# Gated attention product and BitNet feed-forward on one core: FP8 rounding constants made in one step from absolute values, scales moved into PE's diagonals, all four batches of ctx rounded in PSUM

## The chip, the cores and the metric

One Trainium2 chip, one core. The metric is the device time of one execution in microseconds (us). The kernel before has three timed runs, whose median is 73.7 us (73.02 to 74.86), and one profiled execution. The engines are named as in the profile: PE (TensorE), DVE (VectorE), ACT (ScalarE), POOL (GpSimd) and SP (SyncE, which issues all DMAs here).

## The reference, cut to what matters

Input `x` and `ctx` are 4 batches of 256 rows by 256 columns (f32). What is computed:

```
def fp8(t):                      # amax over the whole tensor
    scale = 448 / max(max|t|, 1e-12)
    return float8_e4m3fn(clip(t * scale, -448, 448)) / scale
xn = (x - mean) / sqrt(var + 1e-5)                     # by row
x  = x + tanh(g_xattn) * (fp8(xn) @ fp8(ctx) + mask)    # 256x256 by 256x256, per batch

def bitlinear(x, w, b):
    xn = (x - mean) * rsqrt(var + 1e-5)
    s  = 127 / max(max|xn| by row, 1e-5)
    xq = clip(round(xn * s), -128, 127) / s
    sw = max(mean|w|, 1e-8)
    return xq @ (clip(round(w / sw), -1, 1) * sw).T + b
h = gelu(bitlinear(layernorm(x), w1, b1))              # 256 -> 1024
x = x + tanh(g_ffn) * bitlinear(h, w2, b2)              # 1024 -> 256
```

## The kernel before, in words

Each batch `b` (0 to 3) is 256 rows, two to a partition (`j` = 0, 1); the hidden stage works on eight tiles `t = 2b + j` of 128 rows by 1024. Five queues are written out by hand, in the order in which each engine takes its calls; a call waits on semaphores, and whatever stands behind it on the same engine waits with it. Two-letter tables (`X_BY`, `CQ_BY`, `MX_BY`, ...) say which engine does a step for which batch: A is ACT, D is DVE, P is POOL.

FP8 rounding is done by adding and taking away a constant of the right size for each element (a "magnet"). Before, the value `v` is scaled first (`x_scaled_a`, L570; `ctx_scaled_a`, L576; `ctx_scaled_d`, L796), then DVE takes its exponent bits (`exponent`, L812), then DVE or POOL lifts them to at least LEAST and multiplies by UP, 2^20 (`magnet_d` L817, `magnet_p` L386). PE adds `v`, the magnet and its negative in PSUM with identity matrices. For x (`x_round`, L1060 to L1062) this also transposes: four blocks of three matmuls, one of them f32. For ctx (`ctx_round`, L1069 to L1071) it is three matmuls of 512 columns, for batches 1 and 2; batches 0 and 3 are rounded by DVE (`ctx_rounded`, L822, L824). ACT copies the results out (`xT_out`, `ctx_out`). `first_product` then multiplies, on top of the mask's rows (`mask_in_rows`), and DVE adds the residual and forms the row sum (`first_residual`, L853).

The scales need the largest value of a whole tensor. DVE reduces (`x_part`, `ctx_part`), PE spreads the parts over all partitions (`spread_x`, `spread_c`, with warm-up matmuls `warm` ahead of each), DVE reduces again, and POOL takes the power -1/2 for x (`x_rows_scale`), DVE the reciprocal for ctx.

Then for each batch: ACT squares, DVE largest (`norm_largest`), POOL `norm_mean` and `norm_floor`, DVE `norm_guard`, POOL the powers (`norm_rows`, L420), the rounding to integers (`norm_round_p` L427 or `norm_round_d` L838), DVE `norm_factor` and POOL `scale_parts` (the bias's factor in three bf16 parts), PE's transposes, and `hidden_product`. For each hidden tile: `gelu` and `squares` on ACT, `hidden_largest` on DVE, `hidden_mean` and `hidden_floor` on POOL, `hidden_guard` on DVE, `hidden_rows` (powers, L465) on POOL by the groups of GROUPS, `hidden_round_p` (L474) on POOL, PE's transposes, copies `hT_out` (DVE or ACT), `out_product`, and `second_residual` on DVE, after which SP stores the tile. The last tile's rounding is split between POOL and DVE. POOL also rounds the weights (`weight_round_p`, L400) and adds the output bias (`residual_out_p`, L448).

Of the kernel before, what the change touches and what calls it, by code (L numbers as in the profile page):

```python
# [27 lines left out]


def gated_fp8_bitnet(nc, x, ctx, mask, g_x, g_f, w1, b1, w2, b2, out):  # L30
# [46 lines left out]
    with ExitStack() as es:  # L77
# [247 lines left out]
        def _(pool):  # L325
# [27 lines left out]
            def x_rows_std():  # L353
                pool.wait_ge(x_ve_done, 1)
                pool.tensor_tensor(x_rstd[:, :, :].rearrange("p b j -> p (b j)"),
                                   x_ve[:, :, :].rearrange("p b j -> p (b j)"), minus_half[:, :], ALU.pow)\
                    .then_inc(x_rstd_done, 1)

            def x_rows_scale():
                pool.wait_ge(amax_x_done, 1)  # L360
                pool.tensor_tensor(scale_x[:, :], amax_x[:, :], minus_half[:, 0:1], ALU.pow).then_inc(scale_x_done, 1)
                pool.wait_ge(scale_x_done, 1)
                pool.wait_ge(x_rstd_done, 1)
                pool.tensor_scalar(x_rs[:, :, :].rearrange("p b j -> p (b j)"),
                                   x_rstd[:, :, :].rearrange("p b j -> p (b j)"), scale_x[:, 0:1], 1.0,
                                   ALU.mult, ALU.mult).then_inc(x_rs_done, 1)
                pool.wait_ge(x_rs_done, 1)
# [918 lines left out]
```

## Time and profile before

| | |
|---|---|
| median of 3 runs | 73.7 us (73.02 to 74.86) |
| profiled execution, its own time | 72.76 us |
| its span, first to last instruction | 71.0 us |
| PE, DVE, ACT, POOL busy | 58.5, 57.1, 50.8, 48.4 us |
| DMA | 5.49 MB, nearly all reads in the first 16 us |

Busy time is counted per engine over the span; register, branch and semaphore instructions aren't in it. Where an engine is blocked inside an instruction, the profile counts that as busy, so a duration that is longer than the same operation's elsewhere is worth a look at what another engine did meanwhile.

### The profile page before, as it was taken

To read this page: it belongs to the slowest core of one execution; us is meant where nothing else is said; L and a number is where in the kernel's file an instruction comes from. 1 tells how busy PE (TensorE), PEld (TensorE's weight loads), DVE (VectorE), ACT (ScalarE), POOL (GpSimd) and SP (SyncE) were. 2 spreads that over 40 slices of the span, in tenths; PEclk is the share of its full clock that TensorE was granted. 3 is DMA by queue.
4 is the path that set the end of the run, shared out by engine and by line. 5 is a ranking of instruction groups with operands and counts; after the bars stand their busy time and mean duration, and the time that the engine had idled before them with its cause. 6 is when DMAs were issued, how large, how long until landed. Compare 5 with 4: busy or idle time off the path is not lost. (4 is left out here: it accounts for less than half of the span.)

```text
span 71.0 us, 1599 instructions
## 1 busy us (share of the span) xinstructions
PE 58.5 (83%) x523; PEld 39.5 (56%) x528; DVE 57.1 (80%) x133; ACT 50.8 (72%) x108; POOL 48.4 (68%) x90
## 2 busy tenths in 40 slices
PE   0069999988932899999998998999979999978850
PEld 0069999755931495936383342522756548856730
DVE  1339999778999855989949899469999999999850
ACT  5169922899993475195999797999859997975400
POOL 4012167679999986689996869799507898988100
DMA  0999999951000000000000000000002002102232
GB/s 2 259 247 368 321 327 370 404 158 6 3 1 0 0 0 18 0 0 0 0 5 0 0 0 0 0 0 9 0 0 74 0 0 83 60 14 74 79 133 84
DMA packets 6191, 5.49 MB, mean 77 GB/s; under 512 B 2084, under 2 KB 5544, under 8 KB 6184
## 3 DMA queue, kind: packets, MB, share of 16 engines
q1 hardware_dynamic: 6184, 5.40, 24.6%
q8 instruction: 4, 0.07, 0.4%
q14 instruction: 3, 0.02, 0.1%
HBM read 4.33 MB, written 1.05 MB: 76 GB/s over the span
## 5 line engine op out<-in xcount | busy, mean ns | idle before, releaser
L1020 PE MATMUL p_h<-ident_b 128*128 128x128 bf16 x143 | 10.7, 243 | 4.2 <-DVE x_sum L709 4.2
L1020 PEld LDWEIGHTS p_h<-ident_b 128*128 128x128 bf16 x143 | 10.2, 111 | 4.9 <-issue 4.9
L878 DVE TENSOR_REDUCE h_mx<-h_sqv 128x1 f32<-128x1024 f32 x8 | 9.7, 1206 | 0.0
L621 ACT ACTIVATE h<-p_h,s_f 128x1024 f32<-128x1024 f32 x8 | 8.8, 1103 | 1.0 <-PE p_h L1129 0.9
L474 POOL TENSOR_SCALAR hq<-h,h_nm,h_ar 128x1024 int16<-128x1024 f32 (+1 forms) x8 | 9.1, 1139 | 0.4
L629 ACT ACTIVATE h_sqv<-h,h_sum 128x1024 f32<-128x1024 f32 x8 | 9.1, 1141 | 0.1
L1128 PE MATMUL p_h<-w1T,x1qT 128*128 128x512 bf16 x29 | 9.0, 382 | 0.1
L1060 PE MATMUL p_X<-ident_f,v 128*128 128x128 f32 x32 | 6.4, 301 | 0.2 <-DVE magnet L817 0.2
L465 POOL TENSOR_TENSOR h_ar<-h_ge,minus_half 128x4 f32<-128x4 f32 (+1 forms) x5 | 4.5, 896 | 2.9 <-DVE h_ge L884 2.8
L448 POOL TENSOR_TENSOR y<-x,b_gate 128x256 f32<-128x256 f32 x8 | 6.2, 791 | 0.2
L1129 PE MATMUL p_h<-b_rows,uT 9*128 9x512 bf16 x16 | 6.2, 384 | 0.1
L812 DVE TENSOR_SCALAR magnet<-v 128x512 int16<-128x512 int16 x8 | 4.7, 596 | 1.8 <-ACT v L576 1.3
L400 POOL TENSOR_SCALAR wq<-w_sb,w_inv 128x1024 int16<-128x1024 f32 x4 | 5.6, 1412 | 0.7 <-DVE w_inv L769 0.6
L554 ACT ACTIVATE x_sqv<-x_sb,x_sum 128x256 f32<-128x256 f32 x8 | 4.0, 497 | 2.2 <-DVE x_sum L709 2.1
L560 ACT ACTIVATE w_junk<-w_sb 128x1024 bf16<-128x1024 f32 x4 | 4.2, 1050 | 1.7 <-DMA w_sb<-in_L_ffn_w_dram 1.7
L1060 PEld LDWEIGHTS p_X<-ident_f,v 128*128 128x128 f32 x32 | 4.9, 190 | 0.8 <-DVE magnet L817 0.4
L1129 PEld LDWEIGHTS p_h<-b_rows,uT 9*128 9x128 bf16 x16 | 1.4, 90 | 6.8 <-issue 6.8
L606 ACT ACTIVATE s_sqv<-x,s_sum 128x256 f32<-128x256 f32 x8 | 4.0, 501 | 1.1 <-DVE x L853 1.1
L838 DVE TENSOR_SCALAR x1q<-x,s_nm,s_ar 128x256 int16<-128x256 f32 x6 | 3.9, 685 | 1.0 <-POOL s_ar L420 1.0
L1191 PE MATMUL p_A<-w2T,hqT 128*128 128x256 bf16 x32 | 4.2, 273 | 0.5 <-DVE hqT L909 0.5
L339 POOL TENSOR_SCALAR x_nm<-x_sum 128x2 f32<-128x2 f32 x4 | 0.8, 192 | 5.4 <-DVE x_sum L709 3.7
L1079 PE MATMUL p_A<-mask_s,rows_sel 4*128 4x512 f32 x8 | 4.4, 626 | 0.0
(125 smaller groups left out, 153.5 us busy)
## 6 DMA issues: line engine op xcount, KB each, us to landing
w_sb<-in_L_ffn_w_dram SPq DMA_DIRECT2D x4, 512.0 KB, 6.1
ctx_sb<-in_ctx_dram SPq DMA_DIRECT2D x4, 256.0 KB, 4.8
out_dram<-y SPq DMA_DIRECT2D x8, 128.0 KB, 1.7
x_sb<-in_x_dram SPq DMA_DIRECT2D x3, 256.0 KB, 3.7
x_sb<-in_x_dram SPq DMA_DIRECT2D x2, 128.0 KB, 2.2
b_rows<-b_parts SPq DMA_DIRECT2D x9, 2.0 KB, 2.2
b_sb<-in_L_ffn_b_dram SPq DMA_DIRECT2D x1, 128.0 KB, 7.6
b_sb<-in_L_ffn_b_dram SPq DMA_DIRECT2D x1, 4.0 KB, 4.9
```

Source lines behind the costliest of these rows:

```text
L400: pool.tensor_scalar(wq[:, m, n * F:(n + 1) * F], flat, w_inv[:, m:m + 1], 1.0, ALU.mult, ALU.mult)\
L448: pool.tensor_tensor(y[:, b, j], x1[:, b, j], b2_gate[:, :], ALU.add).then_inc(x1b_done["P"], 1)
L465: pool.tensor_tensor(h_ar[:, lo:hi].rearrange("p t e -> p (t e)"), h_ge[:, lo:hi].rearrange("p t e -> p (t e)"), minus_half[:, 0:2 * (hi - ...
L474: pool.tensor_scalar(hq[:, t % HB, 0:cols], h[:, t, 0:cols], h_nm[:, t:t + 1], h_ar[:, t, 0:1], ALU.add, ALU.mult).then_inc(hq_done["P"], 1)
L621: nc.scalar.activation(h[:, t], p_h[t % 2][:, :, :].rearrange("p a n -> p (a n)"), ACT.Gelu, scale=s_f[:, t // J, t % J:t % J + 1], accum_ ...
L629: nc.scalar.activation(h_sqv[:, t % SQ], h[:, t], ACT.Square, bias=h_sum[:, t:t + 1], scale=-float(F), accum_out=h_sq[:, t:t + 1]).then_in ...
L812: V.tensor_scalar(magnet[:, b % 2, m].bitcast(I16), high, EXP_BITS, MANT_HALF, ALU.bitwise_and, ALU.bitwise_or).then_inc((exp_x_done, exp_ ...
L878: V.tensor_reduce(h_mx[:, t:t + 1], h_sqv[:, t % SQ], AX.X, ALU.max).then_inc(h_mx_done, 1)
L1020: M.matmul(bank[:, 0:P], ident_b[:, :], ident_b[:, :], start=True, stop=True)
L1060: M.matmul(p_X[:, part], v[:, b, 0, part], ident_f[:, :], start=True, stop=False)
L1128: M.matmul(p_h[t % 2][:, n], x1qT[:, b, j, k], w1T[:, k, cols], start=(k == 0), stop=False)
L1129: mm = M.matmul(p_h[t % 2][:, n], uT[:, b, j], b1_rows[:, cols], start=False, stop=True)
```

## The change

- The magnet is made in one operation: absolute value (by ACT, or by DVE as a bit mask) of x normed or of ctx as loaded, in bf16 (`size`), times the scale, at least LEAST. The factor UP moves into PE's constants (`up_b`, `nup_b`), the scale into diagonal matrices (`diag_x`, `diag_c`) that take the place of the f32 identity. `xn` is x normed but not scaled, by POOL for batches 0 and 3, ACT for 1, DVE for 2.
- All batches of ctx go through `ctx_round` and `ctx_out`; `ctx_rounded` isn't called.
- x's variances and their powers come in two halves; the floor of amax is an added element of `x_ratio`.
- `norm_guard`, `norm_factor`, `hidden_guard` and `hidden_factor` use `tensor_scalar` by column where they used two tensor operands.
- Weight roundings: three of four go to DVE. `norm_round` of batches 1 and 2 goes to POOL. `hT_out(3)` goes to ACT. The first hidden group is split into two.
- The orders of the four compute queues are written anew.

The core of the diff, with the helpers of each engine:

```
-EXP_BITS = 0x7F80
-MANT_HALF = 0x0040
+NO_SIGN = 0x7FFF
 UP = float(2**20)
+LEAST_AMAX = (FP8_EPS / FP8_MAX) ** 2
...
-    GROUPS = ((0, 2), (2, 4), (4, 6), (6, 7), (7, 8))
-    HEAD_WARM = 95
-    X_BY = "AAAA"
-    C_BY = "DAAA"
-    CQ_BY = "DAAD"
-    W_BY = "PPPP"
-    NR_BY = "PDDD"
-    MX_BY = "DDDD"
-    MC_BY = "PPDD"
+    GROUPS = ((0, 1), (1, 2), (2, 4), (4, 6), (6, 7), (7, 8))
+    HEAD_WARM = 68
+    X_BY = "PADP"
+    SX_BY = "AADA"
+    SC_BY = "AAAA"
+    CQ_BY = "AAAA"
+    W_BY = "PDDD"
+    NR_BY = "PPPD"
+    MX_BY = "DDPP"
+    MC_BY = "PPPD"
-    WO_BY = "DDAD"
+    WO_BY = "ADAD"
...
 (POOL)
-            def magnet_p(b, m):
-                pool.wait_ge((exp_x_done, exp_c_done)[m], b + 1)
-                pool.tensor_scalar(magnet[:, b % 2, m], magnet[:, b % 2, m], LEAST, UP, ALU.max, ALU.mult)
+            def x_normed_p(b):
+                pool.wait_ge(x_rstd_done, b // XH + 1)
+                pool.wait_ge(x_nm_done, b + 1)
+                for j in range(J):
+                    pool.tensor_scalar(xn[:, b, j * D:(j + 1) * D], x_sb[:, b, j], x_nm[:, b, j:j + 1], x_rstd[:, b, j:j + 1],
+                                       ALU.add, ALU.mult).then_inc(xn_done["P"], 1)
+            def x_scale():
+                pool.wait_ge(raw_x_done, 1)
+                pool.tensor_tensor(scale_x[:, :], amax_raw[:, 0:1], minus_half[:, 0:1], ALU.pow).then_inc(scale_x_done, 1)
+            def magnet_x_p(b):
+                pool.wait_ge(scale_x_done, 1)
+                pool.wait_ge(size_x_done[SX_BY[b]], nth(SX_BY, b))
+                if b >= 2:
+                    pool.wait_ge(xT_psum, b - 1)
+                pool.tensor_scalar(magnet[:, b % 2, 0], size[:, b, 0], scale_x[:, 0:1], LEAST, ALU.mult, ALU.max)\
+                    .then_inc(magnet_done[0]["P"], 1)
...
 (ACT)
+            def size_x_a(b):
+                act.wait_ge(xn_done[X_BY[b]], J * nth(X_BY, b))
+                nc.scalar.activation(size[:, b, 0], xn[:, b], ACT.Abs).then_inc(size_x_done["A"], 1)
+            def size_c_a(b):
+                act.wait_ge(ctx_in[b], 16)
+                nc.scalar.activation(size[:, b, 1], ctx_sb[:, b].rearrange("p k d -> p (k d)"), ACT.Abs)\
+                    .then_inc(size_c_done["A"], 1)
...
 (DVE)
-            V.tensor_scalar(nident_b[:, :], ident_f[:, :], -1.0, None, ALU.mult)
+            V.tensor_scalar(up_b[:, :], ident_f[:, :], UP, None, ALU.mult)
+            V.tensor_scalar(nup_b[:, :], ident_f[:, :], -UP, None, ALU.mult)
...
+            def diagonal_x():
+                dve.wait_ge(scale_x_done, 1)
+                V.tensor_scalar(diag_x[:, :], ident_f[:, :], scale_x[:, 0:1], None, ALU.mult).then_inc(diag_x_done, 1)
...
+            def size_x_d(b):
+                dve.wait_ge(xn_done[X_BY[b]], J * nth(X_BY, b))
+                V.tensor_scalar(size[:, b, 0].bitcast(I16), high_half(xn[:, b]), NO_SIGN, None, ALU.bitwise_and)
...
-                high = v[:, b, m].bitcast(I16).rearrange("p (n e) -> p n e", e=2)[:, :, 1]
-                V.tensor_scalar(magnet[:, b % 2, m].bitcast(I16), high, EXP_BITS, MANT_HALF,
-                                ALU.bitwise_and, ALU.bitwise_or).then_inc((exp_x_done, exp_c_done)[m], 1)
...
             def norm_guard(b):
-                V.scalar_tensor_tensor(out=s_ge[:, b, 0], in0=s_mx[:, b], scalar=1.0 / (float(D) * Q_MAX) ** 2,
-                                       in1=s_ge[:, b, 1], op0=ALU.mult, op1=ALU.max).then_inc(s_g_done, 1)
+                for j in range(J):
+                    V.tensor_scalar(s_ge[:, b, 0, j:j + 1], s_mx[:, b, j:j + 1], 1.0 / (float(D) * Q_MAX) ** 2,
+                                    s_ge[:, b, 1, j:j + 1], ALU.mult, ALU.max).then_inc(s_g_done, 1)
...
 (PE)
-                    M.matmul(p_X[:, part], v[:, b, 0, part], ident_f[:, :], start=True, stop=False)
-                    M.matmul(p_X[:, part], magnet[:, b % 2, 0, part], ident_b[:, :], start=False, stop=False)
-                    mm = M.matmul(p_X[:, part], magnet[:, b % 2, 0, part], nident_b[:, :], start=False, stop=True)
+                    M.matmul(p_X[:, part], xn[:, b, part], diag_x[:, :], start=True, stop=False)
+                    M.matmul(p_X[:, part], magnet[:, b % 2, 0, part], up_b[:, :], start=False, stop=False)
+                    mm = M.matmul(p_X[:, part], magnet[:, b % 2, 0, part], nup_b[:, :], start=False, stop=True)
...
-                M.matmul(p_C, ident_f[:, :], v[:, b, 1], start=True, stop=False)
+                M.matmul(p_C, diag_c[:, :], ctx_sb[:, b].rearrange("p k d -> p (k d)"), start=True, stop=False)
+                M.matmul(p_C, up_b[:, :], magnet[:, b % 2, 1], start=False, stop=False)
+                M.matmul(p_C, nup_b[:, :], magnet[:, b % 2, 1], start=False, stop=True).then_inc(c_psum, 1)
...
-            warm(16, p_h[1][:, 1])
+            warm(38, p_h[1][:, 1])
             spread_c()
-            warm(18, p_h[1][:, 1])
+            x_round(0)
```

The new orders, as far as the prediction speaks of them:

```
POOL: x_mean(0..3), x_rows_std(0), x_normed_p(0), bias_parts, x_scale, x_rows_std(1), x_normed_p(3), magnet_c_p(0),
  mask_scaled, x_rows_shift, magnet_c_p(1), magnet_x_p(2), gated_bias, weight_round_p(0,0), magnet_c_p(2), norm_mean(0),
  residual_out_p(0), norm_floor(0), magnet_x_p(3), norm_rows(0), norm_round_p(0), scale_parts(0), residual_out_p(1),
  norm_floor(1), norm_mean(1), norm_rows(1), residual_out_p(2), norm_round_p(1), scale_parts(1), norm_mean(2),
  norm_floor(2), hidden_mean(0), hidden_mean(1), hidden_floor(0), norm_rows(2), norm_round_p(2), scale_parts(2),
  hidden_rows(0), hidden_round_p(0), ..., hidden_round_p(6), hidden_rows(5), hidden_round_p(7)
ACT: ..., x_squares(3), size_c_a(0), size_c_a(1), gates_tanh, size_c_a(2), size_x_a(0), weight_abs(0,0), size_c_a(3),
  weight_abs(0,1), weight_abs(1,0), xT_out(0), weight_abs(1,1), ctx_out(0), x_normed_a(1), size_x_a(1), size_x_a(3),
  norm_squares(0), weight_out_a(0,0), ctx_out(1), ..., gelu(7), hT_out(3), squares(7), hT_out(4), ...
DVE: ..., x_part, ctx_largest(1), largest_x, ctx_largest(2), ctx_largest(3), diagonal_x, ctx_part, magnet_x_d(0),
  largest_c, diagonal_c, unscaling, x_normed_d(2), size_x_d(2), weight_scale(0), weight_round_d(0,1), weight_scale(1),
  first_residual(0), magnet_x_d(1), weight_round_d(1,0), weight_round_d(1,1), norm_largest(0), norm_guard(0),
  magnet_c_d(3), norm_factor(0), first_residual(1), ...
PE: warm(68), spread_x, warm(38), spread_c, x_round(0), weight_sums(0), ctx_round(0), mask_in_rows(0),
  weight_sums(1), first_product(0), ctx_round(1), weight_T(0,0), x_round(1), mask_in_rows(1), x_round(2),
  first_product(1), ctx_round(2), mask_in_rows(2), norm_T(0), weight_T(0,1), first_product(2), scale_T(0),
  weight_T(1,0), weight_T(1,1), hidden_product(0), hidden_product(1), ctx_round(3), norm_T(1), x_round(3),
  scale_T(1), mask_in_rows(3), first_product(3), norm_T(2), hidden_product(2), ...
```

Warm matmuls in the hidden stage are 14, 19, 6 and 4 where they were 5, 12, 15, 10 and 3.

## Rows read from the trace of the kernel before

**Rows 1.** The page: busy time by engine, and the weight roundings on POOL.
```profile
PE 58.5 (83%) x523; PEld 39.5 (56%) x528; DVE 57.1 (80%) x133; ACT 50.8 (72%) x108; POOL 48.4 (68%) x90
...
L400 POOL TENSOR_SCALAR wq<-w_sb,w_inv 128x1024 int16<-128x1024 f32 x4 | 5.6, 1412 | 0.7 <-DVE w_inv L769 0.6
```

**Rows 2.** The chain that ended last: start us, us, what.
```profile
64.30 0.67 POOL h_ar L465
```

**Rows 3.** List of waits: waiting group, releaser, us in total, times, longest.
```profile
POOL h_ar L465 <- DVE h_ge L884: 2.8, 2, 2.6
...
POOL u_parts L435 <- DVE s_u L874: 1.3, 3, 0.5
...
POOL wq L400 <- DVE w_inv L769: 0.6, 1, 0.6
...
POOL magnet L386 <- DVE magnet L812: 0.4, 1, 0.4
```

**Rows 4.** Timeline of POOL: start us, us, line, operation, and idle before it.
```profile
12.87 0.55 POOL L361 TENSOR_TENSOR scale_x<-amax_x,minus_half 128x1 f32<-128x1 f32 x1 [0.53 <-DVE amax_x L743]
...
13.53 0.28 POOL L364 TENSOR_SCALAR x_rs<-x_rstd,scale_x 128x8 f32<-128x8 f32 x1
...
25.66 1.04 POOL L420 TENSOR_TENSOR s_ar<-s_ge,minus_half 128x4 f32<-128x4 f32 x1
...
26.82 1.09 POOL L427 TENSOR_SCALAR x1q<-x,s_nm,s_ar 128x256 int16<-128x256 f32 x2
...
31.10 0.66 POOL L439 CAST u_parts<-s_rest 128x6 bf16<-128x6 f32 x1
...
47.28 2.37 POOL L474 TENSOR_SCALAR hq<-h,h_nm,h_ar 128x1024 int16<-128x1024 f32 x2
...
61.76 0.70 POOL L465 TENSOR_TENSOR h_ar<-h_ge,minus_half 128x2 f32<-128x2 f32 x1
...
62.83 1.19 POOL L474 TENSOR_SCALAR hq<-h,h_nm,h_ar 128x1024 int16<-128x1024 f32 x1
...
65.07 0.77 POOL L474 TENSOR_SCALAR hq<-h,h_nm,h_ar 128x512 int16<-128x512 f32 x1
```

**Rows 5.** The tile magnet: duration ns min/median/max, first and last start us.
```profile
L386 POOL TENSOR_SCALAR magnet<-magnet x2: 1918/1922/1927, 15.2 to 21.4; 128x512 bf16<-128x512 bf16 x2
...
L812 DVE TENSOR_SCALAR magnet<-v x8: 410/478/1259, 14.6 to 32.7; 128x512 int16<-128x512 int16 x8
...
L817 DVE TENSOR_SCALAR magnet<-magnet x6: 275/372/714, 16.6 to 34.5; 128x512 bf16<-128x512 bf16 x6
...
L822 DVE TENSOR_TENSOR v<-v,magnet x2: 672/682/692, 17.2 to 30.3; 128x512 f32<-128x512 f32 x2
...
L824 DVE TENSOR_TENSOR cq<-v,magnet x2: 691/1090/1490, 17.9 to 31.0; 128x512 bf16<-128x512 f32 x2
```

**Rows 6.** Two source lines of DVE, s_f and x1q: columns as in rows 5.
```profile
L872 DVE TENSOR_TENSOR s_f<-s_t,s_ar x4: 160/161/1061, 29.7 to 47.4; 128x2 f32<-128x2 f32 x4
...
L838 DVE TENSOR_SCALAR x1q<-x,s_nm,s_ar x6: 395/616/1201, 36.4 to 49.7; 128x256 int16<-128x256 f32 x6
```

**Rows 7.** Timeline of DVE: columns as in rows 4.
```profile
21.93 0.47 DVE L853 SCALAR_TENSOR_TENSOR x<-p_A,coef,x_sb 128x256 f32<-128x256 f32 x1
...
28.48 0.47 DVE L853 SCALAR_TENSOR_TENSOR x<-p_A,coef,x_sb 128x256 f32<-128x256 f32 x1
...
63.12 0.91 DVE L884 SCALAR_TENSOR_TENSOR h_ge<-h_mx,h_ge 128x1 f32<-128x1 f32 x1
```

**Rows 8.** Timeline of PE: columns as in rows 4.
```profile
4.18 7.39 PE L1020 MATMUL p_h<-ident_b 128*128 128x128 bf16 x95 [4.18 <-DVE x_sum L709]
...
17.35 0.49 PE L1060 MATMUL p_X<-ident_f,v 128*128 128x128 f32 x2 [0.24 <-DVE magnet L817]
...
23.32 1.12 PE L1069 MATMUL p_hT<-v,ident_f 128*128 128x512 f32 x2 [1.56 <-POOL magnet L386]
...
42.74 0.38 PE L1129 MATMUL p_h<-b_rows,uT 9*128 9x512 bf16 x1
```

More of the change, by code:

```diff
@@ L47, in gated_fp8_bitnet @@
     SQ = 3
+    XH = 2
     HT = 4
@@ L351, in bias_parts, with x_rows_std @@
                 pool.tensor_copy(b1_parts[:, 2], b1_rest[:, 1]).then_inc(b1_ready, 1)
[L353 to L367, printed above, removed]
+            def x_rows_std(i):
+                part = slice(i * XH, (i + 1) * XH)
+                pool.wait_ge(x_ve_done, i + 1)
+                pool.tensor_tensor(x_rstd[:, part].rearrange("p b j -> p (b j)"), x_ve[:, part].rearrange("p b j -> p (b j)"),
+                                   minus_half[:, 0:XH * J], ALU.pow).then_inc(x_rstd_done, 1)
@@ L480, in _ @@
             x_mean(3)
-            x_rows_std()
+            x_rows_std(0)
+            x_normed_p(0)
             bias_parts()
-            x_rows_scale()
+            x_scale()
+            x_rows_std(1)
+            x_normed_p(3)
+            magnet_c_p(0)
             mask_scaled()
-            magnet_p(0, 1)
+            x_rows_shift()
+            magnet_c_p(1)
+            magnet_x_p(2)
+            gated_bias()
             weight_round_p(0, 0)
-            weight_round_p(0, 1)
-            gated_bias()
@@ L489, in _ @@
-            magnet_p(1, 1)
+            magnet_c_p(2)
+            norm_mean(0)
             residual_out_p(0)
             norm_floor(0)
-            norm_mean(0)
+            magnet_x_p(3)
             norm_rows(0)
             norm_round_p(0)
-            weight_round_p(1, 0)
             scale_parts(0)
-            weight_round_p(1, 1)
+            residual_out_p(1)
+            norm_floor(1)
             norm_mean(1)
-            norm_floor(1)
-            residual_out_p(1)
             norm_rows(1)
+            residual_out_p(2)
@@ L502, in _ @@
+            norm_round_p(1)
+            scale_parts(1)
+            norm_mean(2)
             norm_floor(2)
[L503 to L504 removed]
+            hidden_mean(0)
+            hidden_mean(1)
+            hidden_floor(0)
             norm_rows(2)
[L506 removed]
+            norm_round_p(2)
             scale_parts(2)
[L508 to L512 removed]
@@ L513, in _ @@
-            hidden_rows(0)
-            norm_rows(3)
-            hidden_mean(1)
-            hidden_round_p(0)
-            hidden_round_p(1)
-            scale_parts(3)
-            hidden_floor(1)
-            hidden_rows(1)
-            hidden_mean(2)
+            hidden_rows(0)
+            hidden_round_p(0)
+            norm_floor(3)
+            hidden_floor(1)
+            norm_mean(3)
+            norm_rows(3)
+            hidden_rows(1)
+            hidden_round_p(1)
+            hidden_mean(2)
@@ L691, in _ @@
             gelu(7)
+            hT_out(3)
             squares(7)
```

376 lines of the change are left out of this document (196 added, 180 removed).

## The prediction

> **What bounds the kernel now.** I read the page first [rows 1]: PE and DVE are busiest at 83% and 80%, ACT 72%, POOL 68%, and no engine is full, so no single one explains 71.0 us. Then the chain of waits. It is short; what it shows is the end [rows 2]: the last row statistics on POOL start at 64.30 and release the last rounding, the last transposes and the last output products. So the end is set by when POOL gets to `hidden_round_p(7)`. The list of waits and POOL's timeline give the reason. POOL is in-order, and from `x_scale` at 12.87 us to the end of the last rounding at 65.84 [rows 4] it has seven waits: 0.4, 0.6, three of 1.3 together and two of 2.8 together [rows 3], 5.2 by the unrounded timeline. Its 53.0 us there are thus 47.8 us of work. The other limiter is DVE, which hands POOL its inputs: the longest wait, 2.6 us, is for `hidden_guard(1)`, behind a DVE queue that runs back to back.
>
> The DVE rows also show a lock between the two. `s_f` (two operands in SBUF, 2 elements) takes 0.16 us alone and 1.06 us when it starts 0.1 us into a POOL rounding; `x1q` is 0.40 alone and up to 1.20 [rows 6, 4]. The last guard takes 0.91 and ends at 64.03, as `hidden_round_p(6)` does [rows 7, 4].
>
> **The change, by part, on each queue.**
>
> DVE loses eight exponents (median 0.48) and six `magnet_d` (median 0.37), of which three shorter ones come back (0.3) [rows 5]: 3.8 + 2.2 - 0.9 us. It loses both `ctx_rounded`, whose second halves are 0.69 and 1.49 [rows 5] and the first about 0.7 each: 3.6. Two of three `norm_round_d` pairs go, 2 x 2 x 0.62 [rows 6]: 2.5, and `hT_out(3)` and one `ctx_scaled_d`, about 1.0. It gains three weight roundings of 1024 elements; the 256-element `x1q` is 0.40 alone, the 1024 by the same 2 elements a cycle about 0.8, so 2.4 (up to 1.9 each if POOL holds the port); `x_normed_d(2)` 0.8, `size_x_d(2)` 0.4, and some six small diagonals and copies, 1.0. Net -7.6 us, most of it before 36 us; on the path it is worth only what DVE was late for. Guards and factors take the form with one SBUF tensor and scalars. I cost them at 0.17 however POOL stands, and if I am wrong they stay at up to 0.9. The last one saves 0.2 only, since POOL was in `hidden_round_p(6)` until 64.02 and started the row statistics at 64.30 [rows 4, 2].
>
> PE: `ctx_round` for batches 0 and 3 is new, 1.4 us each by the spacing of the one at 23.32 [rows 8]; x rounding keeps its twelve matmuls. The first runs where PE waits now, the other between `hidden_product(1)` and `(2)`. Warm-up ahead of `spread_x` falls from 95 matmuls in 7.39 us [rows 8] to 68 in 5.3, ending at 9.4; `spread_x` now waits for `x_part`, which I put at 10.8. The 38 behind it end at 14.1 and hold up `spread_c` (`ctx_part` is there at 13.3), so ctx's scale moves from 13.7 to 15.2. The x side gains: `x_round(0)` needs only `scale_x` and starts near 14.4, not 17.35 [rows 8].
>
> ACT gives three `ctx_scaled_a` and six x rows (4.9) for seven Abs copies (4.4), of which five need no scale and lie in its idle time ahead of the weight sums. It gains `ctx_out(0)`, `ctx_out(3)`, `weight_out_a(0, 0)` (0.5, 0.5, 0.9) and `hT_out(3)`, 1.0 us between `gelu(7)` and `squares(7)`. `hidden_round_p(6)` on POOL hides the last as long as POOL is the later one; with POOL early it is what is late next. SP's order stays; `bias_parts`, which releases its nine row copies, ends near 12.3 in both.
>
> POOL is where I make the sum, start to start:
> - `x_rows_std(0)` from 8.75 (1.0), `x_normed_p(0)` 1.1, `bias_parts` 1.35, so `x_scale` starts at 12.35, not 12.87: -0.5;
> - `x_rows_std(1)` 1.1 and `x_normed_p(3)` 1.1 (durations of `s_ar` and `x1q` [rows 4]), less `x_rs` 0.36: +1.8;
> - five magnets where there were two, 1.92 [rows 5] and 0.08 between starts: +6.0;
> - one weight rounding where there were four in 5.6 us [rows 1]: -4.5;
> - `norm_round_p(1)` and `(2)`: +2 x 1.15 = +2.3 [rows 4];
> - the first hidden group split, two powers of 0.70 [rows 4] for one of 1.03, and one more mean and floor: +1.0.
>
> That is +6.1. Against it stand the 5.2 us of waits, which must all vanish. I followed the queues: POOL reaches `norm_mean(0)` at 26.3, its input is there at 22.0; `norm_rows(0)` at 30.5, guard ready at 28.6; `norm_rows(1)` 36.2; `norm_rows(2)` 42.5; `hidden_round_p(0)` 46.7 (before 47.28 [rows 4]). I found no wait. So +0.9 to +1.0: the last rounding ends near 66.8, and what follows it is as before.
>
> **The disputed price** is a POOL magnet. The nearest row is `magnet_p`: same shape, same types, also a maximum and a product, 1.92 us both times [rows 5]. The other bound comes from POOL's f32 roundings: 0.77 for 512 elements, 0.55 for 256, 1.19 for 1024 [rows 4]. The new form has the product first and a scale from SBUF, as they do. I take 1.92 since shape, types and the maximum are shared; both ends stay in the range.
>
> The rows show 1.92 us for 512 bf16 elements. The Trainium skill ("GPSIMD Engine Reference", section 3.1) gives about 1.8 cycles an element in the best case, 769 ns for 512 elements. By it five magnets would cost 3.8 and not 9.6. This case's magnet row disagrees with it, its f32 row agrees.
>
> **Conversion.** The profiled execution took 72.76 us for its span of 71.0. The median of the three runs is 73.7, 1.3% above. +1.0 gives 73.8, and at the same ratio 74.7.
>
> **Rivals.**
> 1. *POOL magnets are cheap* (0.77, 5 x 1.15 less, so POOL's queue could end 4.8 earlier than now). Then `magnet_c_p(0)` ends at 16.1, `first_product(0)` at 19.5, `first_residual(0)` starts at 19.6 against 21.93 [rows 7]. POOL doesn't bound any more: `squares(7)` behind the moved `hT_out(3)`, and PE's hidden products with 43 warm matmuls, put the last rounding near 62.5, -3.3. The weight roundings collide with POOL on the port, so I take -2.8: 70.0 profiled, 70.9. For it: the f32 rows. Against: the magnet row.
> 2. *Slower: the magnet ahead of `norm_rows(0)`.* `magnet_x_p(3)` stands in POOL's queue between `norm_floor(0)` and `norm_rows(0)`. At 2.0 us each `norm_rows(0)` starts at 30.5 where it was 25.66 [rows 4]. On DVE `norm_factor(0)` waits for it with `first_residual(1)` behind, 32.1 against 28.48 [rows 7]. PE's `mask_in_rows(2)` waits for that; `hidden_product(0)` and `(1)` end at 37.9 and 39.6, then `ctx_round(3)`, `x_round(3)`, mask and product (4.5 us) lie before `hidden_product(2)`, which ends at 46.6 against 43.1 [rows 8]. If the hidden stage then keeps its old pace and absorbs nothing, it is +3.5 less 0.7 from unlocked guards: 75.6, or 76.6. It decides from the point where POOL waits over 0.5 us in total after 48 us. For it: the old stage had the 2.6 us wait. Against: the sum leaves POOL no time to wait in.
> 3. *It does little*: DVE's two-operand work no longer holds POOL up (`u_parts` is 0.66 beside it [rows 4]), about 1.0 us back from POOL's durations, which cancels the sum: 73.7.
>
> That lock is by instruction in the rows: 0.16 becomes 1.06. The Trainium skill ("SBUF — State Buffer", on the shared pair) says whichever of a DVE 2-port operation and a GpSimd one starts first holds it throughout. That speaks against weight roundings on DVE beside POOL's magnets. In the trace DVE's magnets range from 0.28 to 0.71 [rows 5], so a collision costs up to what POOL has left.
>
> **How the numbers follow.** Forecast 74.7: 0.35, its own range 73.4 to 76.0. Rival 1, 70.9: 0.32; I give it that much since one differing operand may put the new form on the cheap side. Rival 2, 76.6: 0.25. Rival 3, 73.7: 0.08. A difference under 2% (72.2 to 75.2) can't be told from none here. Faster: nearly all of rival 1 and a little of the forecast, 0.34. Slower: most of rival 2 and the upper part of the forecast, 0.31. Within: the rest, 0.35. The range reaches to both ends: 70.2 to 76.9.
>
> **What would show it.** POOL's magnet rows: 1.9 or 0.8. `x_scale` at 12.4, `x_round(0)` at 14.4, `norm_rows(0)` at 30.5 (rival 1: about 25), `hidden_product(2)` ending at 46.6 or 40.6. POOL's waits after 13 us: near none in the forecast, over 0.5 in rival 2. The last guard at 0.2. Wrong would be a first `x_round` later than 15.5, or a queue held up by ACT's Abs copies, which I costed at nothing.

## The result, and the profile after

The changed kernel took 78.75 us (median of four runs, 78.06 to 79.24), the kernel before 73.36 (72.94 to 74.86) in the runs beside it: a ratio of 1.0725 [1.064, 1.0811]. It is 7% slower, beyond the range of the prediction. Runs of one kernel differ by some per cent with the granted clock, so each ratio here and below compares only the least disturbed runs of both sides, while medians and ranges are of all runs. The profiled execution took 78.55 us for a span of 76.4. The mean granted clock of TensorE (1.00 is 2.4 GHz throughout) was 0.933 in every run of it; in the profiled run of before it was 1.00.

The page of the changed kernel: span, busy times, the row of the granted clock in 40 slices, and the costliest group that is new.

```profile
span 76.4 us, 1564 instructions
...
PE 64.1 (84%) x492; PEld 40.7 (53%) x497; DVE 49.4 (65%) x140; ACT 52.6 (69%) x110; POOL 54.4 (71%) x101
...
PEclk9999999999555699999569999999999999999999
...
L400 POOL TENSOR_SCALAR magnet<-size,scale_c 128x512 bf16<-128x512 bf16 x3 | 6.6, 2186 | 0.3
```

Against [rows 1]: DVE did lose its work (57.1 to 49.4 us), POOL took on 6.0 us, and PE's busy time rose by 5.6 us, though it has 31 matmuls fewer (492). The clock row has two dents, one in slices 11 to 14 and one in 20 and 21.

POOL's timeline (start, duration, instruction; in brackets the idle time before it and who ended it).

```profile
12.76 0.56 POOL L382 TENSOR_TENSOR scale_x<-amax_raw,minus_half 128x1 f32<-128x1 f32 x1
...
15.60 2.07 POOL L400 TENSOR_SCALAR magnet<-size,scale_c 128x512 bf16<-128x512 bf16 x1
...
18.95 1.99 POOL L400 TENSOR_SCALAR magnet<-size,scale_c 128x512 bf16<-128x512 bf16 x1
21.03 1.99 POOL L389 TENSOR_SCALAR magnet<-size,scale_x 128x512 bf16<-128x512 bf16 x1
...
24.78 2.50 POOL L400 TENSOR_SCALAR magnet<-size,scale_c 128x512 bf16<-128x512 bf16 x1
...
29.30 1.99 POOL L389 TENSOR_SCALAR magnet<-size,scale_x 128x512 bf16<-128x512 bf16 x1
31.38 1.03 POOL L433 TENSOR_TENSOR s_ar<-s_ge,minus_half 128x4 f32<-128x4 f32 x1
...
37.25 1.03 POOL L433 TENSOR_TENSOR s_ar<-s_ge,minus_half 128x4 f32<-128x4 f32 x1 [0.73 <-DVE s_ge L922]
...
44.03 0.19 POOL L466 TENSOR_SCALAR h_nm<-h_sum 128x1 f32<-128x1 f32 x1 [1.52 <-ACT h L646]
45.16 0.19 POOL L471 TENSOR_SCALAR h_ge<-h_sq 128x1 f32<-128x1 f32 x1 [0.94 <-ACT h_sqv L654]
45.44 1.03 POOL L433 TENSOR_TENSOR s_ar<-s_ge,minus_half 128x4 f32<-128x4 f32 x1
...
49.41 1.20 POOL L487 TENSOR_SCALAR hq<-h,h_nm,h_ar 128x1024 int16<-128x1024 f32 x1
...
58.81 1.03 POOL L478 TENSOR_TENSOR h_ar<-h_ge,minus_half 128x4 f32<-128x4 f32 x1 [1.29 <-DVE h_ge L945]
...
70.29 1.03 POOL L487 TENSOR_SCALAR hq<-h,h_nm,h_ar 128x512 int16<-128x512 f32 x1
```

Three things are to be seen. The five magnets take 2.0 to 2.5 us each. From 13.3 to 36.5 us POOL has no wait at all, so whatever stands in its queue ahead of `norm_rows(0)` is paid in full: that starts at 31.38, against 25.66 [rows 4]. And from 36.5 on POOL does wait: 0.73, 1.52, 0.94 and 1.29, together 4.5 us. The last rounding starts 5.2 later than before (70.29 against 65.07 [rows 4]), which is nearly all of the 5.4 us by which the span grew.

How the lateness travels is on the other queues. DVE's timeline:

```profile
15.92 0.82 DVE L838 TENSOR_SCALAR xn<-x_sb,x_nm,x_rstd 128x256 f32<-128x256 f32 x2
...
32.45 0.45 DVE L929 TENSOR_SCALAR s_t<-s_ge,s_ar 128x1 f32<-128x1 f32 x2 [2.31 <-POOL s_ar L433]
...
33.29 0.48 DVE L911 SCALAR_TENSOR_TENSOR x<-p_A,coef,x_sb 128x256 f32<-128x256 f32 x1
```

and PE's:

```profile
14.18 0.40 PE L1115 MATMUL p_X<-diag_x,xn 128*128 128x128 f32 x2
...
17.81 1.10 PE L1125 MATMUL p_hT<-ctx_sb,diag_c 128*128 128x512 f32 x2 [0.83 <-POOL magnet L400]
...
19.31 2.07 PE L1135 MATMUL p_A<-mask_s,rows_sel 4*128 4x512 f32 x2
...
34.33 1.09 PE L1135 MATMUL p_A<-mask_s,rows_sel 4*128 4x512 f32 x2 [1.92 <-DVE x L911]
...
37.12 1.89 PE L1103 MATMUL p_h<-ident_b,wq 128*128 128x128 bf16 x16
...
42.32 0.39 PE L1185 MATMUL p_h<-b_rows,uT 9*128 9x512 bf16 x1
...
49.34 0.39 PE L1185 MATMUL p_h<-b_rows,uT 9*128 9x512 bf16 x1
```

`norm_factor(0)` on DVE waits 2.31 us for POOL's `s_ar`, with `first_residual(1)` behind it: 33.29 against 28.48 [rows 7]. `mask_in_rows(2)` on PE waits 1.92 us for that. `hidden_product(2)` ends at 49.7 against 43.1 [rows 8].

The same two `mask_in_rows` matmuls take 2.07 us at 19.31 and 1.09 at 34.33: the first run at half the clock. Windows of the changed kernel (start:end, us; busy us and instructions of PE, PEld, DVE, ACT and POOL; granted clock; DMA share; GB/s):

```profile
13.00:36.50 23.50, 20.13 (x126) 12.56 (x124) 12.39 (x41) 13.97 (x29) 21.96 (x28) 0.85 0.16 50
...
20.00:22.00 2.00, 2.00 (x6) 0.69 (x5) 0.00 (x0) 1.97 (x5) 1.91 (x2) 0.50 0.03 1
...
34.00:40.00 6.00, 5.67 (x39) 3.35 (x39) 3.56 (x13) 4.34 (x11) 4.95 (x11) 0.72 0.02 4
```

From 13.0 to 36.5 PE did 126 matmuls in 20.1 us busy at a mean clock of 0.85; before had 165 in 19.93 at 1.00. A busy share read without the clock column would make PE look loaded, when it was slow. Ahead of the first fall (2.4 to 1.2 GHz) PE had worked little between 15.9 and 17.8 us, waiting 0.52 us for a weight's absolute values and 0.83 for the first ctx magnet; ahead of the second it had waited 1.92 us.

So two theories stand for what comes after: the POOL magnets lengthen an unbroken queue and the rest follows (theory 1), or the clock makes much of the loss itself (theory 2). A third is that it matters where one magnet stands (rival 2's `magnet_x_p(3)` just ahead of `norm_rows(0)`).

### The profile page after: what moved, and what is told of

The parts are those of the page before. It is cut to its first block, busy times and chain, and to the rows that moved or that the text cites. A ratio compares the mean times of both kernels' runs of the same rounds, so it can differ in the third digit from the quotient of the medians.

```text
span 76.4 us, 1564 instructions
## 1 busy us (share of the span) xinstructions
PE 64.1 (84%) x492; PEld 40.7 (53%) x497; DVE 49.4 (65%) x140; ACT 52.6 (69%) x110; POOL 54.4 (71%) x101
## 4 chain that ended last, share of the span: by engine, by line
PE 42%; POOL 21%; issue 11%; DMA 9%; SPq 7%; DVE 3%; ACT 2%; POOLq 2%
PE p_h L1184 11%; DMA w_sb<-in_L_ffn_w_dram 9%; PE p_h L1185 7%; POOL magnet L400 6%; POOL magnet L389 3%; PE p_h L1103 3%; PE p_A L1135 3%; POOL hq L487 3%; PE p_X L1074 3%; PE p_X L1247 2%; PE p_A L1247 2%; SPq L310 2%; POOL h_ar L478 2%; PE p_hT L1196 2%; SPq L308 2%
## 5 line engine op out<-in xcount | busy, mean ns | idle before, releaser
L1074 PE MATMUL p_h<-ident_b 128*128 128x128 bf16 x106 | 8.5, 257 | 4.3 <-DVE x_sum L742 4.3
L1074 PEld LDWEIGHTS p_h<-ident_b 128*128 128x128 bf16 x106 | 8.2, 118 | 4.2 <-issue 4.2
L1135 PE MATMUL p_A<-mask_s,rows_sel 4*128 4x512 f32 x8 | 5.4, 760 | 1.9 <-DVE x L911 1.9
L400 POOL TENSOR_SCALAR magnet<-size,scale_c 128x512 bf16<-128x512 bf16 x3 | 6.6, 2186 | 0.3
L1115 PE MATMUL p_X<-diag_x,xn 128*128 128x128 f32 x32 | 6.4, 302 | 0.0
L1125 PE MATMUL p_hT<-ctx_sb,diag_c 128*128 128x512 f32 x8 | 5.2, 732 | 0.8 <-POOL magnet L400 0.8
L478 POOL TENSOR_TENSOR h_ar<-h_ge,minus_half 128x2 f32<-128x2 f32 (+1 forms) x6 | 4.9, 811 | 1.3 <-DVE h_ge L945 1.3
L461 POOL TENSOR_TENSOR y<-x,b_gate 128x256 f32<-128x256 f32 x8 | 5.6, 725 | 0.0
L1115 PEld LDWEIGHTS p_X<-diag_x,xn 128*128 128x128 f32 x32 | 4.8, 191 | 0.8 <-issue 0.8
L433 POOL TENSOR_TENSOR s_ar<-s_ge,minus_half 128x4 f32<-128x4 f32 x4 | 4.1, 1028 | 0.9 <-DVE s_ge L922 0.7
```

Source lines behind the costliest of these rows:

```text
L400: pool.tensor_scalar(magnet[:, b % 2, 1], size[:, b, 1], scale_c[:, 0:1], LEAST, ALU.mult, ALU.max).then_inc(magnet_done[1]["P"], 1)
L478: pool.tensor_tensor(h_ar[:, lo:hi].rearrange("p t e -> p (t e)"), h_ge[:, lo:hi].rearrange("p t e -> p (t e)"), minus_half[:, 0:2 * (hi - ...
L1074: M.matmul(bank[:, 0:P], ident_b[:, :], ident_b[:, :], start=True, stop=True)
L1115: M.matmul(p_X[:, part], xn[:, b, part], diag_x[:, :], start=True, stop=False)
L1135: M.matmul(p_A[:, :, :], rows_sel[:, b], mask_s[:, :].rearrange("b (o n) -> b o n", o=1).broadcast_to([B, J, D]), start=True, stop=True)
```

## Experiments

Each ratio is against runs of the kernel before on the same chip.

**1. All magnets on DVE.** Everything else of the change stays.

```diff
-    MX_BY = "DDPP"
-    MC_BY = "PPPD"
+    MX_BY = "DDDD"
+    MC_BY = "DDDD"
-            magnet_c_p(0)        # and the four others in POOL's queue
+            magnet_c_d(0)        # at the same places of DVE's
```

> The changed kernel with its four POOL magnets of batch 0 to 2 of ctx and two of x (five in all) made by DVE; nothing else. POOL theory: five operations of 2.0 us each stand in POOL's in-order queue, four of them ahead of the row statistics of batch 0 and one right before them; without them norm_rows(0) starts near 25 us instead of 31.4, the second half of hidden_product for tile 2 ends near 43 instead of 49.7, and the time falls from 78.6 by 5 to 7 us, to 72 to 74. Clock theory (PE at half clock from 19 to 26 and 36 to 39 us is what costs): PE still waits between x_round(0) and the mask, the clock falls as before, and no more than 3 us come back.

70.38 us (70.13 to 70.99), ratio 0.9656 [0.95, 0.9812]: faster than before, by 1.9 to 5.0%. It is 8.4 us below the change (7.8 by the ratios), more than either theory expected. Its timeline, POOL and DVE:

```profile
24.93 1.05 POOL L433 TENSOR_TENSOR s_ar<-s_ge,minus_half 128x4 f32<-128x4 f32 x1 [2.51 <-DVE s_ge L917]
...
30.82 1.03 POOL L433 TENSOR_TENSOR s_ar<-s_ge,minus_half 128x4 f32<-128x4 f32 x1 [0.75 <-DVE s_ge L917]
...
37.18 0.19 POOL L471 TENSOR_SCALAR h_ge<-h_sq 128x1 f32<-128x1 f32 x1 [0.94 <-ACT h_sqv L649]
...
50.80 1.03 POOL L478 TENSOR_TENSOR h_ar<-h_ge,minus_half 128x4 f32<-128x4 f32 x1 [1.29 <-DVE h_ge L940]
...
62.24 1.03 POOL L487 TENSOR_SCALAR hq<-h,h_nm,h_ar 128x512 int16<-128x512 f32 x1
...
14.84 0.40 DVE L865 TENSOR_SCALAR magnet<-size,scale_c 128x512 bf16<-128x512 bf16 x1
```

What takes POOL 2.0 us takes DVE 0.4. `norm_rows(0)` comes 6.5 us earlier than in the change, and POOL now waits 2.5 us ahead of it; the clock stays at 1.00 and `hidden_product(2)` ends at 41.7. So the loss goes with where these five instructions are done, and the rest of the change is worth 3.4%. As the clock came back too, this run doesn't separate theories 1 and 2. Three of the changed kernel's waits on POOL are there too (0.75, 0.94, 1.29), though POOL is 6.5 us earlier.

**2. What a POOL magnet costs.** The kernel before, with eight forms of 128x512 `tensor_scalar` at the end of POOL's queue, where the output is being finished.

```diff
+  (t_bo, t_b, sc, LEAST, ALU.mult, ALU.max),     # bf16 -> bf16, the change's form
+  (t_bo, t_b, LEAST, UP, ALU.max, ALU.mult),     # the form of before
+  (t_bo, t_b, sc, 1.0, ALU.mult, ALU.mult),      # no maximum
+  (t_bo, t_f, sc, LEAST, ALU.mult, ALU.max),     # f32 -> bf16
+  (t_fo, t_f, sc, LEAST, ALU.mult, ALU.max),     # f32 -> f32
+  (t_fo, t_f, ...mult, mult), (t_bo, t_f, ...mult, mult), (t_fo, t_b, ...mult, mult)
```

> The kernel before, with eight tensor_scalar operations of 128x512 on scratch tiles behind POOL's last rounding, one after the other: (1) bf16 to bf16, scale times then maximum (the new magnet); (2) bf16 to bf16, maximum then times, both immediates (the old one); (3) bf16 to bf16, times and times; (4) f32 to bf16, times then maximum; (5) f32 to f32, times then maximum; (6) f32 to f32, times and times; (7) f32 to bf16, times and times; (8) bf16 to f32, times and times. If the maximum makes it slow: 1, 2, 4, 5 take 1.9 to 2.0 us and 3, 6, 7, 8 take 0.77. If the bf16 input does: 1, 2, 3, 8 are slow. If the bf16 output does: 1, 2, 3, 4, 7 are slow. Its output is the reference's; its time means nothing.

The eight in this order; the fifth and sixth share a row.

```profile
67.37 2.05 POOL L505 TENSOR_SCALAR t_bo<-t_b,t_s 128x512 bf16<-128x512 bf16 x1
69.51 1.93 POOL L505 TENSOR_SCALAR t_bo<-t_b 128x512 bf16<-128x512 bf16 x1
71.54 0.69 POOL L505 TENSOR_SCALAR t_bo<-t_b,t_s 128x512 bf16<-128x512 bf16 x1
72.33 2.00 POOL L505 TENSOR_SCALAR t_bo<-t_f,t_s 128x512 bf16<-128x512 f32 x1
74.42 2.78 POOL L505 TENSOR_SCALAR t_fo<-t_f,t_s 128x512 f32<-128x512 f32 x2
77.29 0.69 POOL L505 TENSOR_SCALAR t_bo<-t_f,t_s 128x512 bf16<-128x512 f32 x1
78.08 0.69 POOL L505 TENSOR_SCALAR t_fo<-t_b,t_s 128x512 f32<-128x512 bf16 x1
```

The first, second, fourth and fifth have a maximum and take 1.93 to 2.05 us (the fifth alone 1.99); the four without take 0.69, whatever the types. The prediction's two bounds (1.92 from a magnet row, 0.77 from an f32 rounding) differ by the operation and not by the type. Only one shape was tried.

**3. The change without the maximum**, magnets still on POOL (the floor `LEAST` is left out, so tiny inputs are rounded otherwise).

```diff
-  pool.tensor_scalar(magnet[...], size[...], scale[:, 0:1], LEAST, ALU.mult, ALU.max)
+  pool.tensor_scalar(magnet[...], size[...], scale[:, 0:1], 1.0, ALU.mult, ALU.mult)
```

> The changed kernel with every queue as it is; the five POOL magnets only multiply (times scale, times 1.0), the maximum with LEAST is left out, so that the smallest elements are rounded too finely. In the row of forms such an operation took 0.69 us where the one with the maximum took 2.05. If the price of the maximum on POOL is the cause: POOL's queue loses 5 x 1.35 = 6.8 us ahead of the second x rounding and the row statistics, PE's gaps close, the granted clock goes back to 1.00, and the time is that of the version with all magnets on DVE or little above it, 70 to 72. If the placement of the operations on POOL (the lock, the order) costs, most of the 5 us stays lost, 75 or more.

71.89 us (70.93 to 72.31), ratio 0.9778 [0.9703, 0.9854], at a clock of 1.00.

```profile
15.72 0.69 POOL L400 TENSOR_SCALAR magnet<-size,scale_c 128x512 bf16<-128x512 bf16 x1
...
25.40 0.69 POOL L389 TENSOR_SCALAR magnet<-size,scale_x 128x512 bf16<-128x512 bf16 x1 [1.91 <-PE p_X L1117]
26.06 1.05 POOL L433 TENSOR_TENSOR s_ar<-s_ge,minus_half 128x4 f32<-128x4 f32 x1
```

Nothing moves and no order changes; only the price does, and the time falls by 6.9 us, more than the loss. The queue is broken again (a wait of 1.91 us), and PE's waits of 0.83 for the magnet and 1.92 for `x` are gone. With experiments 1 and 2 this shows the cause: the price of the maximum on POOL, times five.

**4. One magnet off POOL: the last or the first.**

```diff
-    MX_BY = "DDPP"                 -    MC_BY = "PPPD"
+    MX_BY = "DDPD"                 +    MC_BY = "DPPD"
-            magnet_x_p(3)          -            magnet_c_p(0)
```

> The changed kernel with magnet_x(3) alone on DVE, behind norm_guard(0); the other four stay on POOL. POOL theory: one operation of 2.0 us less in a queue without a wait up to norm_rows(0), which starts 2.0 earlier (29.4); PE's gap ahead of the mask of batch 2 shrinks from 1.9 us to under 1. 76.0 to 76.8, 1.8 to 2.5 us faster. Clock theory: the first stretch at half clock stays as it is and is most of the loss, so under 1.5 us.

> The changed kernel with magnet_c(0) alone on DVE, behind diagonal_c; the other four stay on POOL. POOL theory: again 2.0 us less in the same unbroken queue, the same 76.0 to 76.8 as with the last magnet moved, though it is another place. Clock theory: this one closes the wait of PE for ctx_round(0) in front of the first stretch at half clock, so it gives clearly more than the last magnet: 75 or less.

Without the last: 75.78 us at a clock of 0.974. Its other runs, at 0.955, 0.933 and 0.934, took 77.35 to 79.1, so no ratio is given; the two at the changed kernel's own clock were no faster than it (79.06 and 79.1 against 78.06 to 79.24). Without the first: 76.94 (75.75 to 77.85), ratio 1.0426 [1.0373, 1.0479], at 0.954 to 0.955.

`norm_rows(0)` starts at 29.60 and 29.17, so 1.8 and 2.2 us before 31.38; 0.4 and 0.5 of that is an earlier `x_scale` (12.36 and 12.23, against 12.76). For this start the place just ahead of `norm_rows(0)` is no worse than the first: each magnet counts with about its length, as it must in a queue without a wait. That is theory 1; the third theory falls. The end doesn't follow so simply. The last rounding starts at 67.74 and 69.59, so 2.6 and 0.7 us before 70.29: in the second profiled execution PE ran at half clock from 32 to 39 us, on the matmuls behind `first_residual(1)`, and that took most of the gain back.

**5. The clock held by spare matmuls.** Two tries. Spare matmuls, whose results nothing reads, go behind `x_round(0)` (10) and `weight_sums(0)` (16), where PE waits, and ahead of `mask_in_rows(2)` (26); the second try has 36 there and 38 more ahead of `weight_T(0, 0)`.

```diff
+            warm(10, p_h[1][:, 1])      # behind x_round(0)
+            warm(16, p_h[1][:, 1])      # behind weight_sums(0)
+            warm(38, p_h[1][:, 1])      # ahead of weight_T(0, 0), second try only
+            warm(26, p_h[1][:, 1])      # ahead of mask_in_rows(2); 36 in the second try
```

> The changed kernel with 10 warm-up matmuls behind x_round(0), 16 behind weight_sums(0) and 26 ahead of mask_in_rows(2), in PE's gaps. If they hold the clock at 1.00 throughout: clock theory says 3 to 4.5 us come back (sum of what PE's rows grew by: about 2.8 in the first stretch, 1.6 in the second), 74 to 75.5. POOL theory says that the first stretch is hidden, since POOL has no wait between 13.3 and 36.5 us, and only the second counts: 1.0 to 1.6 us back, about 77.3.

The first missed: 78.33 us (76.54 to 80.99), and the clock still fell in all but one run (the 76.54). In the profiled one it fell behind a wait of 2.83 us for a weight rounding that I had left uncovered:

```profile
24.96 0.62 PE L1103 MATMUL p_h<-ident_b,wq 128*128 128x128 bf16 x8 [2.83 <-POOL wq L413]
27.84 2.07 PE L1135 MATMUL p_A<-mask_s,rows_sel 4*128 4x512 f32 x2
```

> The changed kernel with warm-up matmuls in all four gaps of PE: 10 behind x_round(0), 16 behind weight_sums(0), 38 ahead of weight_T(0, 0), 36 ahead of mask_in_rows(2). The earlier try left the 2.8 us gap ahead of weight_T(0, 0) open and the clock fell behind it. With the clock at 1.00 throughout: POOL theory 1.5 to 2.2 us back (only the stretch behind 36 us lies on the path; one execution of the earlier try that kept 1.00 took 76.5), 76.4 to 77.1. Clock theory: 4 us or more, 74.5 or less.

The second kept 1.00 in every run: 77.13 us (76.97 to 77.43), ratio 1.0592 [1.0555, 1.0629]. Its POOL timeline:

```profile
12.44 0.56 POOL L382 TENSOR_TENSOR scale_x<-amax_raw,minus_half 128x1 f32<-128x1 f32 x1
...
31.32 1.03 POOL L433 TENSOR_TENSOR s_ar<-s_ge,minus_half 128x4 f32<-128x4 f32 x1
...
47.81 1.20 POOL L487 TENSOR_SCALAR hq<-h,h_nm,h_ar 128x1024 int16<-128x1024 f32 x1
...
68.69 1.03 POOL L487 TENSOR_SCALAR hq<-h,h_nm,h_ar 128x512 int16<-128x512 f32 x1
```

`norm_rows(0)` is where it was (31.32 against 31.38), so the first stretch at half clock was hidden behind POOL. The first hidden rounding and the last both start 1.6 us earlier: the second stretch cost about 1.5, and POOL's wait of 1.52 us for gelu is gone with it. By the ratios the clock is worth 1.0 us (1.0725 less 1.0592, times 73.4; by the ends of the two intervals 0.1 to 1.9). Theory 2 holds for a fifth to somewhat over a quarter of the loss of 5.3 us.

**6. The small forms alone.** The kernel before with the change's guards and factors (one SBUF tensor and scalars).

```diff
-  V.scalar_tensor_tensor(out=s_ge[:, b, 0], in0=s_mx[:, b], scalar=..., in1=s_ge[:, b, 1], ...)
+  for j in range(J):
+      V.tensor_scalar(s_ge[:, b, 0, j:j + 1], s_mx[:, b, j:j + 1], ..., s_ge[:, b, 1, j:j + 1], ...)
   # factors, hidden guards and hidden factors likewise
```

> The kernel before, with the row guards and factors of both norms in the form of the change (tensor_scalar, one column at a time, one SBUF tensor) and nothing else. My costing: each is 0.17 us however POOL stands, so the guards that took 0.86 and 0.91 shrink, and 0.2 us or a little more is gained, 73.2 against 73.4. If the new form is held by POOL too, or two instructions for a pair cost what the lock gave, no gain: 73.4 or up to 0.5 more.

74.96 us (73.89 to 77.26), ratio 1.0145 [0.9889, 1.0401]: unclear, with no gain to be seen. The single-column guards were 0.20 to 0.21, but the factor of two columns with one SBUF tensor reached 0.84 (`s_f`) and 0.48 (`h_f`) beside POOL roundings, against 0.23 elsewhere.

**7. A better order.** From experiment 1: DVE's `norm_largest(0)` and `norm_guard(0)` ahead of the second weight's roundings; on PE `first_product(1)` ahead of `x_round(2)` and `norm_T(0)` ahead of `ctx_round(2)` (ACT's copies in the same order); POOL's `norm_rows(2)` and its rounding ahead of the first hidden means, and DVE's `norm_factor(2)` ahead of `hidden_largest(0)`. The diff shows POOL's part.

```diff
             norm_round_p(1) ...                     # POOL
+            norm_rows(2)
+            norm_round_p(2)
             hidden_mean(0), hidden_mean(1), hidden_floor(0)
-            norm_rows(2)
-            norm_round_p(2)
```

> The version with all magnets on DVE, and these orders: norm_largest(0) and norm_guard(0) ahead of the two roundings of w2 on DVE (POOL waited 2.5 us for that guard); first_product(1) ahead of x_round(2) and norm_T(0) ahead of ctx_round(2) on PE, ACT's copies in the same order; norm_rows(2) ahead of the first hidden means and floor on POOL. If POOL's waits for guards set the pace between 22 and 40 us: the second half of hidden_product for tile 2 ends 1 to 2 us earlier than 41.7, 68.5 to 69.5 against 70.4. If PE's own queue sets it (no gap from 21 us on but 1.5 us), nothing is gained, 70.0 to 70.7.

69.37 us (68.85 to 72.01), ratio 0.946 [0.9355, 0.9564]: with experiment 9's the best version of this study, 4.4 to 6.5% under the kernel before. The last rounding starts at 61.39, not 62.24. Against experiment 1 it gains about 1 us (1.4 by the ratios, whose intervals overlap). What each of the orders gave is open.

**8. Batch 3 of ctx back to DVE**, from experiment 1, and with experiment 7's order.

```diff
-    CQ_BY = "AAAA"
+    CQ_BY = "AAAD"
+            ctx_rounded(3)      # DVE
-            ctx_round(3)        # PE
```

> The version with all magnets on DVE, and batch 3 of ctx rounded by DVE as before the change (two operations of 0.7 us behind first_residual(1), where DVE waits 1.2 us), so that PE has one ctx_round of 1.4 us less between hidden_product(1) and (2). If PE's queue between 21 and 44 us sets the end: 1.0 to 1.4 us faster than 70.4, 69.0 to 69.4. If DVE or POOL does: no gain or up to 0.5 slower.

> Both edits: the reordered queues and batch 3 of ctx on DVE. 68.5 to 69.3 if either limiter theory holds; 70.0 or more if the hidden stage, which takes 20.8 us from the first to the last rounding in every version with the new orders (17.8 before), sets the end by itself.

72.25 us (70.67 to 75.11) and 72.14 (69.07 to 76.68), without ratios: the clock fell in seven of the eight runs (to 0.886 at the least; the only one at 1.00 was the 69.07). Page of the first of the two:

```profile
PEclk9999999999999999999999658999999999999999
```

The one run at full clock, 69.07, lies within experiment 7's three (68.85 to 69.46), so no gain is to be seen. In the first version's trace PE waits 0.98 us for ACT's `x1qT` from 36.26, near the place that `ctx_round(3)` had, and the clock falls at about 38.5. That this fourth ctx rounding in PSUM guards the clock fits this, but only these runs say so, and the clock fell too in four of the seven runs of the kernel before beside them.

**9. The hidden stage's order**, from experiment 7: `squares(3)` ahead of `gelu(4)`; `hidden_largest(3)` and `hidden_guard(2)` ahead of `second_residual(0)` and `hidden_factor(1)`.

```diff
-            gelu(4)
             squares(3)
+            gelu(4)
```

> The reordered version (69.4), and in the hidden stage squares(3) ahead of gelu(4) on ACT, and hidden_largest(3) and hidden_guard(2) ahead of second_residual(0) and hidden_factor(1) on DVE: POOL waits 1.2 us for that guard and then runs without a wait to the end. If that wait sets the end, 0.8 to 1.2 us are gained, 68.2 to 68.6. If PE's queue (33 warm-up matmuls ahead of hidden_T(1), products 6 and 7) is as late, no gain.

69.48 us (69.22 to 70.21), ratio 0.9541 [0.9473, 0.9609]: no gain over experiment 7.

```profile
49.44 1.03 POOL L478 TENSOR_TENSOR h_ar<-h_ge,minus_half 128x4 f32<-128x4 f32 x1 [0.53 <-DVE h_ge L940]
...
52.84 0.19 POOL L471 TENSOR_SCALAR h_ge<-h_sq 128x2 f32<-128x2 f32 x1 [0.80 <-ACT h_sqv L649]
```

POOL's wait for the guard shrank from 1.21 to 0.53, and a new one of 0.80 for the squares took its place.

## Why the prediction was wrong

**The step that failed** is the last of POOL's sum: the 5.2 us of waits "which must all vanish", and "I found no wait". By the forecast's own terms:

| POOL, us | forecast | measured |
|---|---|---|
| start of `x_scale` | -0.5 | -0.1 |
| work from there to the end of the last rounding | +6.6 | +6.3 |
| waits in it | -5.2 | -0.7 |
| end of the last rounding | +0.9 | +5.5 |

The measured work is 71.3 less 12.8 less the 4.5 us of waits, so 54.1 against 47.8. Of the magnets alone the five took 11.0 us start to start and not 10.0; POOL's other work was 1.3 less than forecast. The work was right within 0.3. The error of 4.6 us is 4.5 of waits and 0.4 of the start, less 0.3.

**Why the waits stayed.** A late engine has no waits only while its inputs don't depend on its own late outputs. That holds to 36.5 us. But `norm_rows(0)` releases DVE's factor, with `first_residual(1)` behind it, that releases PE's mask and the hidden products, those ACT's gelu and squares, and POOL waits for these. So its lateness moved its later inputs with it, and what lies behind `norm_rows(0)` could not be shortened by POOL's old waits. Starts in us:

| | `norm_rows(0)` | last rounding | between | POOL's waits over 0.6 between |
|---|---|---|---|---|
| before | 25.66 | 65.07 | 39.4 | 0.64, 2.62 |
| changed | 31.38 | 70.29 | 38.9 | 0.73, 1.52, 0.94, 1.29 |
| clock held (experiment 5) | 31.32 | 68.69 | 37.4 | 0.73, 0.94, 1.28 |
| magnets on DVE (experiment 1) | 24.93 | 62.24 | 37.3 | 0.75, 0.94, 1.29 |

The last two rows differ by 6.4 us at `norm_rows(0)` and by 0.1 behind it. With the new orders this stretch takes 37.3 to 37.4 us at full clock, and 3.0 us of POOL's waits stand in it, whether POOL comes to it early or late; the fourth, 1.52, goes with the clock. The forecast had 35.5 there (from 30.5 to a last rounding of 0.8 that ends at 66.8). So the loss of 5.2 at the last rounding is 5.7 at `norm_rows(0)`, less 2.0 that the new orders save behind it, plus 1.5 of clock.

This is rival 2's mechanism, and its sign came true (POOL waits "over 0.5 us in total after 48 us": 1.29), though 3.2 of the 4.5 us stand ahead of 48. Its figures drift from the trace along the chain: `norm_rows(0)` 30.5 (31.38), `first_residual(1)` 32.1 (33.29), end of `hidden_product(1)` 39.6 (42.71), of `hidden_product(2)` 46.6 (49.73). POOL waited for the gelu behind `hidden_product(1)`; with gelu's 1.2 us behind the rival's own 39.6, next to no wait would have been left there (an estimate: the forecast has POOL at `norm_rows(2)`, just behind, at 42.5). So putting rival 2's times into the forecast would not have mended all of it. Some of the waiting is due to order: `norm_rows(2)` has its guard at 42.6 but starts at 45.44, since `hidden_mean(1)` and `hidden_floor(0)`, on late products, stand ahead of it. Experiment 7 turned this about among other things, so what it alone costs is open.

Rival 2 named the magnet just ahead of `norm_rows(0)`; experiment 4 shows that the first one counts for that start as well. It was also 2.1 us short (76.6 forecast). About 1.0 to 1.5 of that is the clock; 1.2 had come already by `first_residual(1)`. **The clock** stands in no step of the prediction: the profile of before shows 1.00 throughout, and I took its matmul durations as fixed. I named the waits that the change would put on PE and didn't ask what they do to the work behind them.

**The disputed price** was taken rightly (1.92; 2.0 to 2.5 measured), for a reason half right: the types, which I gave beside the maximum, have no part in it (experiment 2); the shape was not varied. Rival 1's 70.9 was a fair account of the other case: without the maximum the kernel takes 71.9. The form without a maximum takes 0.69 us. The Trainium skill ("GPSIMD Engine Reference", section 3.1) gives 769 ns for 512 elements in the best case. The form without a maximum is a little under that; the forms with one take 2.5 to 2.7 times as long.

**Right:** `x_scale` at 12.8 (12.4), `x_round(0)` at 14.2 (14.4), ACT's Abs copies and `hT_out(3)` at no cost (no wait of POOL is for them), DVE's 7.7 us fewer (7.6). **Half right:** the small forms "at 0.17 however POOL stands". The rows of the changed kernel, by source line (count, shortest, median and longest in ns, first and last start):

```profile
L888 DVE TENSOR_SCALAR wq<-w_sb,w_inv x3: 745/752/1092, 17.5 to 25.4; 128x1024 int16<-128x1024 f32 x3
...
L932 DVE TENSOR_SCALAR s_f<-s_t,w_fac x4: 228/254/1103, 32.9 to 53.3; 128x2 f32<-128x2 f32 x4
...
L945 DVE TENSOR_SCALAR h_ge<-h_mx,h_ge x8: 202/213/214, 47.3 to 68.8; 128x1 f32<-128x1 f32 x8
```

One column stays at 0.2 (five of the eight guards ran beside a POOL rounding). Two columns were held to 1.10 beside the hidden rounding that starts at 53.21, as the two-operand form was [rows 6]. The weight roundings took the 0.75 to 0.8 that I gave them, one of them 1.09; none was held for the rest of a 2.0 us magnet. The POOL magnet at 24.78 took 2.50 beside two of them, and 2.00 in experiment 5's second try, where they had ended before it; that fits DVE holding it up. The Trainium skill ("SBUF — State Buffer", section "SBUF: two separate sides") says that of a DVE operation in a 2-port mode and a GpSimd one whichever starts first holds the shared ports throughout. The rows agree for DVE behind a POOL rounding, but not behind a POOL magnet: DVE's two `xn` operations of 256 columns took 0.82 together at 15.92, all within the magnet from 15.60 to 17.67, where an operation of that size took 0.40 alone and up to 1.20 beside a POOL rounding [rows 6].
